# Order of the late guest units, and the places of guests and VectorE exponentials in attention

## The reference, cut to what matters

```python
h = tok(x, W, b, cls)                                        # (4, 3137, 128)
h = h + attn(layernorm(h))                                   # 8 heads of 16, softmax over 3137 keys, plus position bias, @ Wo
y = layernorm(h)
pooled = sum(y * softmax(y @ attn_w + attn_b, tokens))       # per image
gates = softmax(pooled @ gate_w + gate_b); take the best 2 of 8 experts
h = h + sum over 2 experts of g_e * gelu(gelu(y @ w1_e + b1_e) @ w2_e + b2_e)
```

## Time and profile before

| | us |
|---|---|
| median of 3 runs (lowest to highest) | 2872.43 (2869.24 to 2874.86) |
| profiled execution, its own time | 2869.71 |
| span of the trace | 2868.0 |
| PE busy, ACT busy, DVE busy, POOL busy | 2534.1, 2524.5, 1616.4, 873.1 |

### The profile page before, as it was taken

How to read it: one execution, slowest core, us unless ns; L and a number is a source line. 1 busy time by engine, 2 the same in 40 slices (tenths; PEclk the granted TensorE clock), 3 DMA queues, 4 the chain that set the end, 5 groups by cost and what they waited for, 6 DMA issues and landing times.

```text
span 2868.0 us, 123840 instructions
## 1 busy us (share of the span) xinstructions
PE 2534.1 (88%) x55860; PEld 1252.9 (44%) x55860; DVE 1616.4 (56%) x2542; ACT 2524.5 (88%) x2733; POOL 873.1 (30%) x1424
## 2 busy tenths in 40 slices
PE   7988888888888888988889898888989888999897
PEld 3444444444444444444444444444444444555454
DVE  5754777776756556555565565565655654443310
ACT  5669999999999999999999999999999999544453
POOL 2113443333333333333333333333333333100000
PEclk9989999999999999999999999999999999999999
DMA  5540101100101110011111000111110011210010
GB/s 145 172 163 12 38 32 33 32 29 29 41 29 35 32 32 29 29 51 43 30 36 33 29 29 29 51 40 35 32 32 29 29 52 46 91 35 14 14 35 19
DMA packets 65911, 125.43 MB, mean 44 GB/s; under 512 B 10034, under 2 KB 55180, under 8 KB 63892
## 3 DMA queue, kind: packets, MB, share of 16 engines
q1 hardware_dynamic: 63324, 110.93, 12.4%
q0 software_dynamic: 2048, 6.43, 0.6%
HBM read 67.30 MB, written 51.30 MB: 41 GB/s over the span
## 4 chain that ended last, share of the span: by engine, by line
ACT 46%; PE 25%; issue 18%; DVE 6%; DMA 3%; POOL 0%; SPq 0%; ACTq 0%; DVEq 0%; POOLq 0%
ACT shared L897 45%; PE ps L812 6%; PE ps L773 5%; PE ps L781 5%; PE ps L730 3%; PE ps L757 2%; PE ps L727 2%; DMA k_halves<-halves 1%; DVE root L1087 1%; PE ps L669 1%; DVE std L1019 1%; DVE root L1080 1%; DVE root L1078 1%; DVE root L1132 0%; DVE root L1130 0%
## 5 line engine op out<-in xcount | busy, mean ns | idle before, releaser
L897 ACT ACTIVATE shared<-ps 128x1179 f32<-128x1179 f32 (+1 forms) x2167 | 2205.8, 1181 | 34.1 <-PE ps L730 18.3
L812 PE MATMUL ps<-shared,va 64*32 64x393 f32 x25600 | 1565.4, 500 | 1.3 <-issue 0.9
L980 POOL TENSOR_TENSOR shared<-shared,e_all 128x310 f32<-128x310 f32 (+19 forms) x1344 | 814.9, 623 | 1441.5 <-ACT shared L897 1434.5
L730 PE MATMUL ps<-qa,ka 48*32 48x393 f16 (+1 forms) x15200 | 733.8, 319 | 138.3 <-ACT shared L897 122.2
L727 PE MATMUL ps<-qa,ka 51*32 51x393 f16 (+8 forms) x13184 | 658.9, 313 | 122.4 <-ACT shared L897 114.0
L812 PEld LDWEIGHTS ps<-shared,va 64*32 64x32 f32 x25600 | 617.3, 139 | 31.9 <-issue 5.2
L730 PEld LDWEIGHTS ps<-qa,ka 48*32 48x32 f16 x15200 | 242.6, 90 | 603.5 <-ACT shared L897 575.1
L727 PEld LDWEIGHTS ps<-qa,ka 51*32 51x32 f16 x13184 | 218.5, 89 | 641.4 <-ACT shared L897 621.8
L1057 DVE COPY xc<-ps 128x393 f32<-128x393 f32 x64 | 36.4, 569 | 533.2 <-PE ps L812 533.2
L1087 DVE SCALAR_TENSOR_TENSOR root<-root 128x393 f32<-128x393 f32 x486 | 319.6, 658 | 16.7
L916 ACT ACTIVATE qa<-ps,b 128x393 f32<-128x393 f32 x256 | 136.6, 586 | 111.6 <-PE ps L773 111.5
(11 more groups left out here) (149 smaller groups left out, 1629.7 us busy)
## 6 DMA issues: line engine op xcount, KB each, us to landing
qa<-q_halves SPq DMA_DIRECT2D x64, 196.5 KB
ka<-k_halves SPq DMA_DIRECT2D x64, 196.5 KB
att_rows<-std SPq DMA_DIRECT2D x64, 196.5 KB, 4.0
v_rows<-v_sb SPq DMA_DIRECT2D x4, 1600.0 KB, 6.9
va<-v_rows SPq DMA_DIRECT2D x32, 200.0 KB, 15.9
ln_rows<-ln SPq DMA_DIRECT2D x32, 196.5 KB, 5.6
q_halves<-halves SPq DMA_DIRECT2D x32, 196.5 KB, 3.1
k_halves<-halves SPq DMA_DIRECT2D x32, 196.5 KB, 4.3
```

The lines of the kernel that those rows point to most:

```text
L730: last = nc.tensor.matmul(out[x:y, cut:W], ka[r:r + 48, par, k0 + x:k0 + y], qa[r:r + 48, par, q0 + cut:q0 + W], start=True, stop=True, ti ...
L812: last = nc.tensor.matmul(ps[quad:quad + 32, O_PS + half, 0:W], va[r:r + 64, par, :, kt], pr[r:r + 64, g % SLOTS_PR, j], start=(kt == 0), ...
L897: nc.scalar.activation(pr[:, g % SLOTS_PR, 0:m], ps[:, b0:b0 + m, 0:W], ACT.Exp, scale=-1.0 / (LOG2E * LIFT * LIFT)).then_inc(s_exp, 1)
L980: nc.gpsimd.tensor_tensor(p, p, e_all[0:keys, n % HEADS, t:t + z - a], ALU.mult).then_inc(s_biased, 1)
```

## The change

Three constants or lists change; no instruction is added or removed.

```diff
-GUEST_POS = (30, 50, 70)
+GUEST_POS = (30, 54, 78)
...
+def late_order():
+    steps = []
+    for s in range(CH + 3):
+        for kind, lag in (("Y", 0), ("M", 1), ("V", 2), ("S", 3)):
+            if 0 <= s - lag < CH:
+                steps.append((kind, s - lag))
+    return steps + [("G", 0)]
...
-    wanted = [q * PASS + pos for q in range(1, 2 * NBH) for pos in ((33, 53) if q in busy else (28, 46, 64, 82))]
+    wanted = [q * PASS + pos for q in range(1, 2 * NBH) for pos in ((34, 58) if q in busy else (28, 46, 64, 82))]
...
-                return (k // GUESTS,) + guest_list[k % GUESTS]
+                return (k // GUESTS,) + (guest_list if k // GUESTS < B - 1 else late_list)[k % GUESTS]
...
-                return b * GUESTS + guest_list.index((kind, c))
+                return b * GUESTS + (guest_list if b < B - 1 else late_list).index((kind, c))
```

More of the change, by code:

```diff
@@ L409, in build @@
             guest_list = [(kind, c) for kind, c, p, pos in guest_plan()]
-            chunk_pass = {c: p for kind, c, p, pos in guest_plan() if kind == "Y"}
+            late_list = late_order()
             def guest(k):
-                return (k // GUESTS,) + guest_list[k % GUESTS]
+                return (k // GUESTS,) + (guest_list if k // GUESTS < B - 1 else late_list)[k % GUESTS]
             def guest_number(b, kind, c):
-                return b * GUESTS + guest_list.index((kind, c))
+                return b * GUESTS + (guest_list if b < B - 1 else late_list).index((kind, c))
             def expert_unit(U):
```

## The result

The changed kernel takes 2849.97 us (2846.63 to 2851.53) beside 2871.71 us for the one before in the same comparison: a ratio of 0.9922, interval 0.9905 to 0.9939. It is faster, by 22 us. The forecast was 46 us faster, and its range of 2816 to 2842 does not hold the time. The profiled execution of after spans 2845.0 us, 23.0 less than the one of before.

The account below looks back on a forecast made before the run. ACT was taken to pace attention and PE the experts, DVE costing only by making them wait. 2869.7 - 27.4 (late guests) - 19 (attention) = 2823.3 us, plus 2.7 for the median: 2826 us, range 2816 to 2842.

Parts of the forecast that it names:

- Late guests: Experts: in the new order no guest depends on the one ahead, so the old order's whole 27.4 us go.
- The rival of the half clock that stays: Experts: the half-clock stretches stay though the waits go; 7 us less gain, 2833 us; chance 0.08.
- Attention, what goes: Attention: 15.5 us of PE's waits for DVE go, worth say 19 us of time, bounds 13 and 27.4.
- the 19 us: Attention: forecast gain, from 15.5 us of PE's waits for DVE times 1.2, 18.6, say 19 us.
- the 8 that were to show the forecast right: Attention, sign of being right: ACT waiting about 8 us instead of 27.4.
- The factor of 1.2 from PE's waits to ACT's: Attention: each removed PE wait counted 1.2 times for ACT; in three places 3.1 us had become 4.3.
- Rival C: Attention gives nearly nothing, something else being late next, as PE is at nine tenths too; 2845 us; chance 0.08.
- Rival D: Experts: DVE's chain ahead of the accumulation holds ACT, then PE; 27.4 us lost, 2853 us; chance 0.04.
- F: Attention: `plain` puts off D groups, so V may follow closely; about 2838 us; chance 0.04.
- E: Attention: V nearer the next pass's drain makes drain late, over 1.9 us in each of 24 passes; slower; chance 0.03.
- The lower end of the attention term, 13 us: Attention: gain if twelve guests now five groups behind an exponential each cost 0.5 us, 6 us less.

## Why the prediction was right and wrong

Late guests: right. 27.4 us were worked out, 27.1 seen in the trace and 26.7 in the run of that part alone. The rival of the half clock that stays fell, on both sides: after has clock 1.00 over the whole stretch, and with S behind V both waits and slow stretches return. One reading of the new order was wrong and cost nothing: S(c) does not come four units behind V(c) but, by the list, four (c = 0, 5), five (c = 1 to 4), three (c = 6) or two (c = 7). The shortest, 11.9 us, had been reckoned with.

Attention, what goes: right in kind, and the 19 us are borne out only roughly. PE's waits for V, Y and M are gone and 2.0 us of 18.4 are left. In the changed kernel 30 idle stretches worth 23.7 us beside a net loss of 2.8 us leave 21 us for what went. The kernel with the late order alone and the changed one with HOLD 7 differ by 18.1 us (2845.75 and 2827.61). But from first to last exponential HOLD 7 is only 14.5 us shorter than before (2233.2 and 2247.7), and ACT's listed waits fell from 27.4 to 13.7 us, not to the 8 that were to show the forecast right. That HOLD 7 lands within 2 us of the forecast 2826 is in part luck.

The factor of 1.2 from PE's waits to ACT's rests in part on a misreading of pass 19, where PE's 2.1 us were set against ACT's 2.9. ACT in that pass, and a window of it with the granted clock as seventh number, counted from the window's length:

```profile
877.98 1.15 ACT L897 ACTIVATE shared<-ps 128x1179 f32<-128x1179 f32 x1 [0.22 <-PE ps L730]
881.28 3.26 ACT L897 ACTIVATE shared<-ps 128x1179 f32<-128x1179 f32 x3 [2.15 <-PE ps L730]
885.09 4.48 ACT L897 ACTIVATE shared<-ps 128x1179 f32<-128x1179 f32 x4 [0.55 <-PE ps L730]
```

```profile
882.00:885.40 3.40, 3.01 (x64) 1.62 (x64) 3.23 (x6) 2.85 (x4) 2.07 (x3) 0.51 0.02 5
```

PE's wait for the V guest was passed on at about its own length, 2.15 us. The 0.22 us lie ahead of it, and the 0.55 us end a stretch at the lower level of the clock, which began behind PE's wait.

The step that failed is the first sentence of the part on attention: "Counts of groups and of D and guest groups are the same, so ACT's own work is the same; only ACT's waits can go." ACT's own work was the same: from first to last exponential, idle time left out, 2213.6 us before and 2211.4 after. But waits could also come. I treated the move as one of DVE's work alone and went through every pair for DVE's queue. PE's queue was moved too. `turns` is worked out from the same places, and I did not list which turns of PE changed, though the rule with HOLD and D_LAG stood in the code. Of each pair I asked only whether it was far enough apart; seven groups is the one distance at which the batch held for the exponential is due in the guest's own turn. The term for such new waits of ACT for PE stood at nothing; it measured 23.7 us of idle time in 30 places, and 22 us of the kernel's time by HOLD 7.

Rival C had a later bottleneck of scores and values by PE, and with its 2845 us it names the right engine and nearly the time. But it got 0.08, and its mechanism, PE being nearly full on the whole, is not the one that acted: ACT waited 13.7 us instead of 32.9 in attention once 30 turns were emptied by one constant. Rival D (a new wait in the late order) did not occur: PE is busy through all of the late guests. F (the places put off by `plain`) shows in no wait. E (drain) did not cost anything either, since PE waits for drain nowhere in the changed kernel, but it came nearer than was reckoned. Pass 19, with its 7.11 us of idle time ahead of drain, was among the roomiest; over the 24 passes with a V guest the least was 4.3 us before, and after it is under 3 us in twelve and nothing in pass 41. The lower end of the attention term, 13 us, was built from DVE's lateness again, so no width of it could take in a gain below zero.

The sentence from the Trainium skill (GPSIMD Engine Reference, Specifications) that DVE and POOL contend where DVE has two inputs in SBUF changed nothing that can be seen here: the exponential's instructions are nearly as long on the mean as they were (its three of L1087 658 ns before, 664 after). The trace is in line with the sentence itself: of these 486 instructions in the kernel before, the 254 with no instruction of POOL beside them all took under 0.6 us, and the longer ones, up to 1.24, all had one.

## What to carry to other kernels

When a piece of one engine's work is moved in a schedule that other queues are planned from, print the plan of every queue before and after, and compare them slot by slot, not just the queue for which the move is made. A short slot of the pacing engine, here a group of two units, has no room for what an ordinary slot carries; a rule of the form "if older than N" next to a lag of N + 1 makes certain distances collide. Where each engine works through a fixed order, a consumer placed directly behind a long producer holds up all that follows it; here interleaving several chunks by a lag added no wait and gave the whole of the stall back, with the clock.

## What was not expected of the hardware

Short waits of PE can cost more than themselves. Of eight waits of 2.3 us each in the kernel before, four were followed by a stretch in which eight matmuls took about 4.3 us instead of 2.65; so 18.5 us of waits made 27 us of time, there and again with S put back behind V, where again four of eight were slow. The Trainium skill (TensorE: Matmul & The Clock Gate, What's actually happening) says that the clock is gated by idleness and released by activity, and these runs agree; that idle stretches of 2.3 us each could be followed by it, I had from the trace alone. Which ones is not a fixed pattern: the second, fourth, sixth and eighth before, the third, fourth, sixth and eighth with S behind V.
